# First weight tile ahead of x, an absolute sum traded between VectorE and ScalarE, first convolution ahead of x's statistics, and unread products at TensorE's start

## The chip, the cores and the metric

The kernel runs on one NeuronCore of one Trainium2 chip. Five engines work side by side and meet only at semaphores: TensorE (PE, matmuls and transposes), VectorE (DVE), ScalarE (ACT), GpSimd (POOL), and SyncE (SP), which issues nearly all DMAs. The metric is the device time of one execution in microseconds, as a median over several runs.

## The reference

The computation is one Mamba-like mixer followed by one ternary-weight feed-forward block, on x of shape (4, 512, 512).

```python
# mixer, for each of 4 batches; hidden = ctx (512 x 256), z = layernorm(x)
xi    = in_proj_w @ hidden.T                     # 512 channels x 512 steps
u     = silu(causal_conv(xi, conv_w, 4 taps) + conv_b)
dbl   = x_proj_w @ u                             # dt (16), B (16), C (16)
delta = softplus(dt_proj_w @ dt + dt_proj_b)
state = state * exp(delta * A) + delta * u * B   # 16 states, scan over 512 steps
y     = (sum over states of state * C + D * u) * silu(z)
x     = x + y.T
# feed-forward; x and h are rounded to 8 bits by row
w_q   = clip(round(w / mean|w|), -1, 1) * mean|w|   # w_gate, w_up: 2048 x 512; w_down: 512 x 2048
h     = silu(q(layernorm(x)) @ w_gate_q.T) * (q(layernorm(x)) @ w_up_q.T)
out   = x + q(rms_norm(h)) @ w_down_q.T
```

`mean|w|` is one number for each weight matrix. It needs the sum of the absolute values over the whole matrix before any element can be rounded.

## The kernel before

The kernel has three stages. A preparation stage (0 to about 93 us) makes everything that the scan reads. The scan stage runs 64 steps k (4 batches by 16 states); in each, ACT makes four decay tiles (L697) and four B-scaled tiles (L619 or L622), PE turns them (L1229, L1232), DVE does four scans of 128x512 (L929), POOL multiplies all four by C (L475) and PE adds them up (L1245). The feed-forward stage takes 16 tiles of 128 rows. The changed lines all lie in the preparation stage.

Each engine runs its own list of steps in the order in which it is written. A step that waits on a semaphore holds up all that stands behind it on that engine. The lists of the preparation stage are these.

* **SP** loads in_proj_w, ctx of batch 0, the convolution's constants, x of batch 0 (`load_x(0)`, L270), weight tile (0, 2) (`load_weight(0, 2)`, L276), ctx of batch 1 and so on. Weight tile (w, k) is quarter k of matrix w (0 gate, 1 up, 2 down), 128x2048 float32, 1 MB. Later SP stores the rounded tiles to DRAM (`store_weight`, L283) and waits for each rounded tile first.
* **PE** multiplies in_proj_w with ctx (`conv(b, h)`, L1108, two 128x512 results), adds the partial weight sums over the partitions (`total(w)`, L1158), makes dt, B and C (`project(g)`, L1118, batches 2g and 2g+1), delta's argument (`delta_in`, L1133), and turns z and delta*u (`turn_z` L1142, `turn_du` L1152). All of these but the totals and B share three pairs of PSUM banks: a use of a pair waits until the use three places earlier in `UNIT_USERS` has been read. `keep_warm(n)` (L1163) issues n products of `ones` that nothing reads.
* **ACT** takes the last tap of the convolution out of PSUM (`last_tap`, L558), sums weight tiles (`sum_weight`, L574, with an accumulator read behind it), applies silu to u (`silu_u`, L565, after all of a batch's convolution), scales weight tiles (`scale_weight`, L581, after the mean), keeps B (`keep_bT`, L597), applies softplus (L602) and silu to z (L569).
* **DVE** takes x's statistics (`x_stats(b)`, L872, L875, L877), the other three taps (`conv(b, h)`, L840, 6 instructions), sums some weight tiles (`sum_weight`, L847), turns the totals into means (`mean_weight`, L853, L856, L859), rounds and clips weight tiles (`cut_weight`, L864, L867), and copies the turned delta*u out of PSUM (`keep_duT`, L883).
* **POOL** normalises x (L434, L441) and multiplies delta by u (`du(b)`, L451).

Who sums which tile: ACT sums gate (0,2), (0,1), (0,0), (0,3) and up (1,0), (1,3), (1,1); DVE sums up (1,2) and all four of down. `total(w)` waits on the counters of both engines by the numbers in `ACT_SUMMED` and `DVE_SUMMED`:

```python
def total(w):
    hold(pe, "w_summed_act", ACT_SUMMED[w], "w_summed", DVE_SUMMED[w])
```

On PE `total(1)` stands behind `pe.wait_ge(S["bT_ready"], 1)` (ACT's `keep_bT(0)`) and behind `delta_in(0, 1)`, and ahead of `project(1)`.

Of the kernel before, what the change touches and what calls it, by code (L numbers as in the profile page):

```python
# [68 lines left out]
def mixer_ffn(nc, x, ctx_t, in_t, conv_w, conv_b, xp_t, dt_t, dt_b, a_log, d_skip, w_all, ln_w, out):  # L69
    es = ExitStack()  # L70
    with es:
# [29 lines left out]
        def w_full(at):  # L101
            return part(at, 8)
# [83 lines left out]
        S = {n: sem(n) for n in names}  # L186
# [9 lines left out]
        wq_stored = [[sem(f"w{w}_stored{k}") for k in range(4)] for w in range(2)]  # L196
        LAST = NB * DS - 1

        ACT_SUMMED, DVE_SUMMED = (5, 7, 7), (0, 1, 5)
        DVE_CUT, ACT_CUT = ((0, 0), (0, 3), (0, 1), (0, 2), (1, 1), (1, 0), (1, 2)), ((1, 3),)  # L200

        FFN_STEPS = range(TILES)
# [59 lines left out]
        def _(sp):  # L262
            def load(dst, src, s):
                sp.dma_start(dst, src).then_inc(S[s], 16)
# [4 lines left out]
            def load_x(b):  # L269
                sp.dma_start(gate_rows(b), x_v[:, b, :, :]).then_inc(x_loaded[b], 16)  # L270
# [4 lines left out]
            def load_weight(w, k):  # L275
                sp.dma_start(w_full(W_AT[w][k]), w_all[w * 4 + k, :, :]).then_inc(w_loaded[w][k], 16)  # L276
# [16 lines left out]
            load(cw[:], conv_w.rearrange("(k p) n -> p k n", p=P), "conv_loaded")  # L293
            with nc.allow_non_contiguous_dma("one column for each channel"):
                load(cb[:], conv_b.rearrange("(k p) -> p k", p=P), "conv_loaded")
            load_x(0)
            load_weight(0, 2)
            load_ctx(1)
            load_weight(0, 1)
            load_x(1)  # L300
# [249 lines left out]
        def _(act):  # L550
# [11 lines left out]
            def silu_u(b):  # L562
                act.wait_ge(S["conv_steps"], (b + 1) * 12)
                u = flat(delta_u[:, b, 1])
                nc.scalar.activation(u, u, ACT.Silu).then_inc(S["u_ready"], 1)  # L565
# [6 lines left out]
            def sum_weight(w, k):  # L572
                act.wait_ge(w_loaded[w][k], 16)
                own.done(nc.scalar.activation(w_junk, w_full(W_AT[w][k]), ACT.Abs,  # L574
                                              accum_out=wstat[:, w * 4 + k:w * 4 + k + 1]))
                own.wait()
                act.sem_inc(S["w_summed_act"], 1)
# [17 lines left out]
            def keep_bT(g):  # L595
                act.wait_ge(S["bT_psum"], g + 1)
                nc.scalar.activation(bT[:, 2 * g:2 * g + 2, :, :], ps[:, 7, :].rearrange(  # L597
                    "p (k j n) -> p j k n", k=KL, j=2)[:, :, :, B_AT:C_AT], ACT.Copy).then_inc(S["bT_ready"], 1)
# [26 lines left out]
            act.preload_act_table_set("silu_and_others")  # L625
            last_tap(0, 0)
            last_tap(0, 1)
            sum_weight(0, 2)
            last_tap(1, 0)
            sum_weight(0, 1)  # L630
            last_tap(1, 1)
# [16 lines left out]
            scale_weight(0, 3)  # L648
            sum_weight(1, 1)
            silu_u(2)  # L650
            keep_bT(0)
            silu_u(3)
            act.preload_act_table_set("softplus")
# [158 lines left out]
        def _(dve):  # L812
# [17 lines left out]
            def conv(b, h):  # L830
                v = delta_u[:, b, 1, :, :]
                first = (b * 2 + h) * 6
                for i in range(1, TAPS):
                    for j in range(2):
                        k = 2 * h + j
                        if i == 1:
                            dve.wait_ge(S["tap0_done"], (b * 2 + h) * 2 + j + 1)
                        else:
                            dve.wait_ge(S["conv_steps"], first + (i - 2) * 2 + j + 1)
                        nc.vector.scalar_tensor_tensor(  # L840
                            out=v[:, k, i:], in0=two("conv", b, h)[:, j, 0:L - i],
                            scalar=cw[:, k, TAPS - 1 - i:TAPS - i], in1=v[:, k, i:], op0=ALU.mult,
                            op1=ALU.add).then_inc(S["conv_steps"], 1)

            def sum_weight(w, k):
                dve.wait_ge(w_loaded[w][k], 16)
                nc.vector.tensor_reduce(out=wstat[:, w * 4 + k:w * 4 + k + 1], in_=w_full(W_AT[w][k]), axis=AX.X,  # L847
                                        op=ALU.add, apply_absolute_value=True).then_inc(S["w_summed"], 1)
# [20 lines left out]
            def x_stats(b):  # L869
                dve.wait_ge(x_loaded[b], 16)  # L870
                for k in range(KE):
                    own.done(nc.vector.bn_stats(bst_x[:, k, :], x_all[:, b * KE + k, :]))  # L872
                own.wait()
                for k in range(KE):
                    own.done(nc.vector.bn_aggr(mv_x[:, b, k, :], bst_x[:, k, :]))  # L875
                own.wait()
                nc.vector.tensor_scalar(var_x[:, b, :], mv_x[:, b, :, 1], LN_EPS, None,  # L877
                                        ALU.add).then_inc(S["x_var"], 1)

            def keep_duT(b, h):  # L880
                dve.wait_ge(wq_stored[1][b], 16)
                dve.wait_ge(S["duT_psum"], b * 2 + h + 1)
                nc.vector.tensor_copy(turned[:, b, 2 * h:2 * h + 2, :], two("du", b, h)).then_inc(S["duT_ready"], 1)  # L883

            x_stats(0)
            conv(0, 0)
            conv(0, 1)
            x_stats(1)
            conv(1, 0)
# [5 lines left out]
            conv(2, 1)  # L895
            conv(3, 0)
            conv(3, 1)
            sum_weight(1, 2)
            cut_weight(0, 0)
            mean_weight(1)  # L900
            cut_weight(0, 3)
# [191 lines left out]
        def _(pe):  # L1093
# [66 lines left out]
            def keep_warm(n):  # L1160

                for _ in range(n):
                    mm(ps[:, 6, 0:P], ones[:], ones[:], start=True, stop=True)  # L1163

            pe.wait_ge(S["in_loaded"], 16)
            conv(0, 0)
            conv(0, 1)
# [1 line left out]
            conv(1, 1)  # L1169
            conv(2, 0)  # L1170
            conv(2, 1)
            pe.wait_ge(S["dve_consts"], 1)
            total(0)
            conv(3, 0)
            pe.wait_ge(S["proj_loaded"], 16 * 6)
# [197 lines left out]
```

## Time and profile before

| what | value |
|---|---|
| median of 3 runs | 574.37 us (573.48 to 574.68) |
| profiled execution, span from first to last instruction | 572.7 us |
| profiled execution, a time of its own | not listed; the median run is 1.67 us above this span |
| busy in the span: PE, DVE, ACT, POOL | 536.1, 535.1, 513.3, 465.1 us |
| granted TensorE clock, mean | 0.997 |

Several engines are busy for over 90% of the span, so the busy shares alone do not say which of them sets the time in a given stage. What does are the waits: where an engine has none over a long stretch, it is the bound there or runs level with the bound. Where it has one, the length of that wait is the room that this engine had. A row of the timeline gives the start, the length, the engine, the line and the number of merged instructions; in square brackets stands the idle time just before it and who ended it.

### The profile page before, as it was taken

To read this page: it belongs to the slowest core of one execution; us is meant where nothing else is said; L and a number is where in the kernel's file an instruction comes from. 1 tells how busy PE (TensorE), PEld (TensorE's weight loads), DVE (VectorE), ACT (ScalarE), POOL (GpSimd) and SP (SyncE) were. 2 spreads that over 40 slices of the span, in tenths; PEclk is the share of its full clock that TensorE was granted. 3 is DMA by queue.
4 is the path that set the end of the run, shared out by engine and by line. 5 is a ranking of instruction groups with operands and counts; after the bars stand their busy time and mean duration, and the time that the engine had idled before them with its cause. 6 is when DMAs were issued, how large, how long until landed. Compare 5 with 4: busy or idle time off the path is not lost.

```text
span 572.7 us, 10285 instructions
## 1 busy us (share of the span) xinstructions
PE 536.1 (94%) x3667; PEld 403.2 (70%) x3684; DVE 535.1 (93%) x778; ACT 513.3 (90%) x757; POOL 465.1 (81%) x196
## 2 busy tenths in 40 slices
PE   5888988899999999999999889999899999999996
PEld 2335477799998999989899879998344444444443
DVE  3999988999999999999999999999999999999883
ACT  1899999999999999989999899999987878878784
POOL 4889364999999999999999999995757676675772
PEclk9999999999999999999999998999999999999999
DMA  9992591221111832126632257443544344533521
GB/s 279 408 390 76 201 323 36 55 58 57 56 56 56 191 105 93 56 65 123 165 99 63 59 129 188 137 154 97 83 78 96 76 101 84 110 84 71 106 55 74
DMA packets 62194, 68.64 MB, mean 120 GB/s; under 512 B 41137, under 2 KB 41137, under 8 KB 59969
## 3 DMA queue, kind: packets, MB, share of 16 engines
q1 hardware_dynamic: 59776, 63.59, 37.5%
q0 software_dynamic: 2368, 4.40, 4.8%
q8 instruction: 30, 0.49, 0.4%
q14 instruction: 20, 0.16, 0.1%
HBM read 50.02 MB, written 8.52 MB: 102 GB/s over the span
## 4 chain that ended last, share of the span: by engine, by line
PE 36%; ACT 24%; DVE 18%; POOL 9%; issue 7%; DMA 5%; SPq 0%; DVEq 0%; POOLq 0%
PE ps L1280 16%; ACT arena L697 11%; PE ps L1290 9%; POOL arena L475 9%; ACT arena L622 7%; DVE arena L840 5%; PE ps L1245 4%; PE ps L1229 4%; DMA arena<-c_rows 3%; DVE arena L929 3%; ACT arena L619 2%; PE ps L1232 2%; DVE bst_x L872 2%; DMA arena<-x 1%; DVE arena L864 1%
## 5 line engine op out<-in xcount | busy, mean ns | idle before, releaser
L475 POOL TENSOR_TENSOR arena<-arena 128x2048 f32<-128x2048 f32 x63 | 286.7, 4614 | 14.1 <-DVE arena L929 9.8
L929 DVE TENSOR_TENSOR_SCAN arena<-arena,ps 128x512 f32<-128x512 f32 x256 | 286.7, 1197 | 1.7 <-PE ps L1229 0.4
L697 ACT ACTIVATE arena<-arena,a_neg 128x512 f32<-128x512 f32 x256 | 164.8, 711 | 7.9 <-DVE arena L929 7.8
L1245 PE MATMUL ps<-ident,arena 128*128 128x128 f32 x1024 | 154.8, 274 | 5.9 <-POOL arena L475 3.7
L1245 PEld LDWEIGHTS ps<-ident,arena 128*128 128x128 f32 x1024 | 119.9, 141 | 9.7 <-POOL arena L475 5.3
L1280 PE MATMUL ps<-arena 128*128 128x512 bf16 x497 | 112.5, 379 | 3.6 <-DVE arena L1006 2.2
L1229 PE MATMUL ps<-arena 128*128 128x128 f32 x768 | 103.4, 278 | 3.9 <-DVE arena L929 3.8
L512 POOL TENSOR_TENSOR arena<-arena 128x1024 f32<-128x1024 f32 x30 | 71.0, 2366 | 39.9 <-DVE arena L1006 39.7
L622 ACT ACTIVATE arena<-arena,bT 128x512 f32<-128x512 f32 x160 | 102.0, 710 | 0.0
L1232 PE MATMUL ps<-ident,arena 128*128 128x128 f32 x640 | 96.0, 273 | 3.0 <-ACT arena L622 2.1
L1229 PEld LDWEIGHTS ps<-arena 128*128 128x128 f32 x768 | 94.5, 194 | 5.8 <-ACT arena L622 2.7
L1280 PEld LDWEIGHTS ps<-arena 128*128 128x128 bf16 x512 | 49.7, 98 | 63.6 <-DVE arena L1006 2.7
L1232 PEld LDWEIGHTS ps<-ident,arena 128*128 128x128 f32 x640 | 74.2, 141 | 5.6 <-issue 3.0
L1290 PE MATMUL ps<-arena 128*128 128x512 bf16 x254 | 57.6, 379 | 0.6 <-DVE arena L1079 0.3
L781 ACT ACTIVATE arena<-arena,magic,aq 128x2048 f32<-128x2048 f32 x14 | 29.3, 2095 | 21.9 <-DVE aq L970 21.9
L1290 PEld LDWEIGHTS ps<-arena 128*128 128x128 bf16 x256 | 24.9, 98 | 30.4 <-DVE arena L1079 0.5
L749 ACT ACTIVATE arena<-ps,scales 128x512 f32<-128x512 f32 x64 | 41.8, 678 | 4.0 <-PE ps L1280 3.1
L1006 DVE TENSOR_TENSOR arena<-arena,ps 128x512 f32<-128x512 f32 x64 | 43.5, 681 | 0.6 <-ACT arena L749 0.3
L1108 PE MATMUL ps<-arena 128*128 128x512 f32 x64 | 31.3, 640 | 8.9 <-DMA arena<-ctx_t 8.0
L993 DVE TENSOR_REDUCE half_max<-arena 128x1 f32<-128x1024 f32 x30 | 36.5, 1216 | 2.5 <-DVE var L954 0.5
L441 POOL TENSOR_SCALAR arena<-arena,mv_x,rstd_x 128x512 f32<-128x512 f32 x16 | 33.0, 2076 | 0.4
L840 DVE SCALAR_TENSOR_TENSOR arena<-ps,cw,arena 128x511 f32<-128x511 f32 (+2 forms) x48 | 31.8, 739 | 0.0
(122 smaller groups left out, 574.8 us busy)
## 6 DMA issues: line engine op xcount, KB each, us to landing
arena<-w_all SPq DMA_DIRECT2D x16, 1024.0 KB, 9.2
arena<-c_rows SPq DMA_DIRECT2D x64, 256.0 KB, 3.3
arena<-x SPq DMA_DIRECT2D x4, 1024.0 KB, 16.0
w_ternary<-arena SPq DMA_DIRECT2D x8, 512.0 KB, 4.1
arena<-w_ternary SPq DMA_DIRECT2D x8, 512.0 KB, 4.8
arena<-x POOLq DMA_DIRECT2D x4, 1024.0 KB, 10.6
out<-arena SPq DMA_DIRECT2D x16, 256.0 KB, 2.0
arena<-ctx_t SPq DMA_DIRECT2D x4, 512.0 KB, 14.0
```

The source lines that it names most:

```text
L475: nc.gpsimd.tensor_tensor(hs[:, k % RING, :, :], hs[:, k % RING, :, :], c_bc[:, s:s + 1, :].to_broadcast([P, KE, L]), ALU.mult).then_inc(S ...
L512: nc.gpsimd.tensor_tensor(p2[:, s, w], h2[:, s, w], lnw[:, w], ALU.mult).then_inc(S["p2_ready"], 1)
L622: nc.scalar.activation(dB[:, slot(k), i, :], turned[:, b, i, :], ACT.Copy, scale=bT[:, b, i, n:n + 1]).then_inc(S["dB_ready"], 1)
L697: nc.scalar.activation(dA[:, s, i, :], delta_u[:, b, 0, i, :], ACT.Exp, scale=a_neg[:, i, n:n + 1]).then_inc(S["dA_ready"], 1)
L840: nc.vector.scalar_tensor_tensor(out=v[:, k, i:], in0=two("conv", b, h)[:, j, 0:L - i], scalar=cw[:, k, TAPS - 1 - i:TAPS - i], in1=v[:, k ...
L929: nc.vector.tensor_tensor_scan(out=hs[:, k % RING, i, :], data0=dA[:, k % 2, i, :], data1=ps[:, 4 + i, :], initial=0.0, op0=ALU.mult, op1= ...
L1006: nc.vector.tensor_tensor(h2[:, t % 2, j * 512:(j + 1) * 512], sg[:, j % 2, :], ps[:, U_BANK[(t * 4 + j) % 3], :], ALU.mult).then_inc(S["h ...
L1229: last = mm(to, turned[:, k // DS, c, i * P:(i + 1) * P], dgB[:, slot(k), c, :], start=True, stop=True)
L1232: last = nc.tensor.transpose(to, dB[:, slot(k), c, i * P:(i + 1) * P], ident[:])
L1245: last = mm(ps[:, c, i * P:(i + 1) * P], hs[:, k % RING, i, c * P:(c + 1) * P], ident[:], start=(n == 0 and i == 0), stop=(n == DS - 1), i ...
L1280: last = mm(ps[:, bank, :], q1T[:, t, c, :], w[:, c, j * 512:(j + 1) * 512], start=(c == 0), stop=(c == KE - 1))
L1290: last = mm(ps[:, DOWN_BANK[t % 2], :], q2T[:, t % 2, c, :], wd(c), start=(c == 0), stop=(c == KI - 1))
```

## The change

Five things change.

1. SP issues weight tile (0, 2) ahead of x of batch 0. The two loads trade places; both are 1 MB.
2. The sum of tile (0, 2) moves from ACT (behind its first two `last_tap`) to DVE, as DVE's first step on loaded data.
3. DVE does `conv(0, 0)` ahead of `x_stats(0)`.
4. The sum of tile (1, 2) moves from DVE (behind `conv(3, 1)`) to ACT, between `silu_u(2)` and `keep_bT(0)`. The counts on which `total` waits follow.
5. PE starts with 12 products that nothing reads, once `ones` is set. The wait for it moves from ahead of `total(0)` to the start.

```diff
-        ACT_SUMMED, DVE_SUMMED = (5, 7, 7), (0, 1, 5)
+        ACT_SUMMED, DVE_SUMMED = (4, 7, 7), (1, 1, 5)
@@ SP
+            load_weight(0, 2)
             load_x(0)
-            load_weight(0, 2)
             load_ctx(1)
@@ ACT
             last_tap(0, 0)
             last_tap(0, 1)
-            sum_weight(0, 2)
             last_tap(1, 0)
@@
             sum_weight(1, 1)
             silu_u(2)
+            sum_weight(1, 2)
             keep_bT(0)
             silu_u(3)
@@ DVE
+            sum_weight(0, 2)
+            conv(0, 0)
             x_stats(0)
-            conv(0, 0)
             conv(0, 1)
@@
             conv(3, 1)
-            sum_weight(1, 2)
             cut_weight(0, 0)
             mean_weight(1)
@@ PE
+            pe.wait_ge(S["dve_consts"], 1)
+            keep_warm(12)
             pe.wait_ge(S["in_loaded"], 16)
             conv(0, 0)
@@
             conv(2, 1)
-            pe.wait_ge(S["dve_consts"], 1)
             total(0)
```

## Rows read from the trace of the kernel before

**Rows 1.** The chain that ended last, in order of time: start us, us, what.
```profile
2.80 8.15 DMA arena<-x
10.98 2.48 DVE bst_x L872 x4
54.98 2.19 DVE wstat L847
73.47 4.75 DMA w_ternary<-arena
```

**Rows 2.** DMA issues at 1.2, 2.8 and 3.3 us; last column is us to landing.
```profile
arena<-ctx_t SPq DMA_DIRECT2D x1, 512.0 KB, 4.7
arena<-x SPq DMA_DIRECT2D x1, 1024.0 KB, 8.2
arena<-w_all SPq DMA_DIRECT2D x1, 1024.0 KB, 10.8
```

**Rows 3.** DVE in the timeline, 10 to 182 us.
```profile
10.98 2.47 DVE L872 BATCH_NORM_STATS2 bst_x<-arena 128x6 f32<-128x512 f32 x4 [8.12 <-DMA arena<-x]
...
36.17 4.01 DVE L840 SCALAR_TENSOR_TENSOR arena<-ps,cw,arena 128x511 f32<-128x511 f32 x6
...
57.09 1.22 DVE L864 TENSOR_SCALAR arena<-arena 128x2048 bf16<-128x2048 f32 x1
...
58.95 0.15 DVE L853 TENSOR_REDUCE wsum<-ps 128x1 f32<-128x4 f32 x1
...
91.15 2.36 DVE L883 COPY arena<-ps 128x1024 f32<-128x1024 f32 x2 [0.23 <-PE ps L1152]
...
93.42 82.40 DVE L929 TENSOR_TENSOR_SCAN arena<-arena,ps 128x512 f32<-128x512 f32 x74
```

**Rows 4.** ACT in the timeline, 27 to 175 us.
```profile
27.14 1.91 ACT L574 ACTIVATE arena<-arena 128x2048 bf16<-128x2048 f32 x1 [0.98 <-DMA arena<-w_all]
...
37.64 4.08 ACT L581 ACTIVATE arena<-arena,magic,winv 128x2048 f32<-128x2048 f32 x2
...
50.97 1.89 ACT L574 ACTIVATE arena<-arena 128x2048 bf16<-128x2048 f32 x1
52.77 0.19 ACT L574 ACTIVATION_READ_ACCUMULATOR arena<-arena 128x1 f32 x1
53.08 1.91 ACT L565 ACTIVATE arena<-arena 128x2048 f32<-128x2048 f32 x1
...
56.97 1.28 ACT L653 ACT_TABLE_LOAD   x1
...
82.46 1.03 ACT L569 ACTIVATE arena<-ps 128x1024 f32<-128x1024 f32 x1 [0.88 <-PE ps L1142]
...
90.73 2.56 ACT L697 ACTIVATE arena<-arena,a_neg 128x512 f32<-128x512 f32 x4
...
170.05 2.55 ACT L697 ACTIVATE arena<-arena,a_neg 128x512 f32<-128x512 f32 x4
```

**Rows 5.** All waits of ACT, 27.2 to 96 us: total us, times, longest.
```profile
ACT arena L569 <- PE ps L1142: 0.9, 1, 0.9
ACT arena L602 <- PE ps L1133: 0.3, 1, 0.3
```

**Rows 6.** PE in the timeline, 6 to 92 us.
```profile
6.13 16.62 PE L1108 MATMUL ps<-arena 128*128 128x512 f32 x32 [6.13 <-DMA arena<-ctx_t]
...
57.32 0.35 PE L1158 MATMUL ps<-wstat,ones 128*128 128x4 f32 x2 [0.24 <-DVE wstat L847]
...
88.06 1.06 PE L1152 MATMUL ps<-ident,arena 128*128 128x128 f32 x8 [0.17 <-ACT arena L569]
...
89.95 1.97 PE L1152 MATMUL ps<-ident,arena 128*128 128x128 f32 x16 [0.70 <-POOL arena L451]
```

**Rows 7.** The first convolution's operand loads on PE, a slow and a fast one.
```profile
9.68 0.34 PEld L1108 LDWEIGHTS ps<-arena 128*128 128x128 f32 x1 [0.52 <-issue]
...
12.32 0.19 PEld L1108 LDWEIGHTS ps<-arena 128*128 128x128 f32 x1 [0.24 <-issue]
```

## The prediction

> **What bounds the kernel now.** I read the chain of waits first, from the start to 93 us, because every changed line lies there. The reader is to see that it goes through x's first load, then through DVE with hardly a break from 10.98 to 73.47 us, then through a store of a rounded weight tile [rows 1]. Read alone, it says that DVE sets the preparation stage, and that DVE's wait of 8.12 us for x [rows 3] is the place to put work. The change does that.
>
> The second view is the timeline of ACT, with its waits listed. From 27.14 us, where it waits 0.98 us for weight tile (1,0) [rows 4], to 96 us ACT waits twice: 0.31 and 0.88 us [rows 5]. So ACT is not off the path, it runs one step behind it. The 0.31 us is no room: the product it waits for needs a PSUM pair that ACT's own softplus empties, so that wait moves along with ACT. The room of ACT over 60 us is the 0.88 us ahead of 82.46.
>
> The third view is the start of the scans. DVE scans from 93.42 us without a wait, 74 scans in 82.40 us [rows 3]. ACT is ahead of it there: its first decay tiles start at 90.73, so the first is done near 91.4, 2.0 us before the first scan. The tiles of step 18 start at 170.05 [rows 4], and the scans of step 18 begin two scans before the stretch ends, at 175.8 - 2 x 1.11 = 173.6, so they are ready 2.9 us ahead. DVE's first scan, not ACT's first decay, carries the delay to the end, and behind it nothing has a time of its own that could absorb it: every load and store there is released by scans or products. The price of the change is therefore how far 93.42 moves.
>
> **The change part by part.**
>
> *Loads traded.* x lands at 2.80 + 8.15 = 10.95, tile (0,2) at 3.35 + 10.8 = 14.15 [rows 1, 2]. Both move 1 MB, they land in the order of issue, and the bytes ahead of every later load are the same, so tile (1,0) still lands at 27.1. After the trade (0,2) lands in x's place and x at about 14.15. From 5.9 us (ctx at 1.25 + 4.7) x's megabyte took 5.0 us, beside small loads of constants; the weight's took 3.2. The two bounds of the landing are 5.95 + 3.2 = 9.15, and 14.15 if the trade does nothing. I take 10.75, near the row of x, since the small loads stay where they are.
> The Trainium skill, "DMA: Bandwidth & Descriptors", section "Queues, rings and completion order", says that descriptors of one queue on an engine are consumed in ring order, yet completion is not first in, first out. The two landings, 3.2 us apart in the order of issue [rows 1, 2], agree with the ring order. By ring order alone the traded tile lands near 10.95; if completions slipped past one another, near 14.15, which is the third rival below.
>
> *Sum of (0,2) on DVE, convolution ahead of statistics.* One sum is 2.19 us [rows 1]. DVE starts at 10.75 instead of 10.98 and gets 2.19 longer before everything up to the old place of sum (1,2). So all of it comes 2.19 - 0.2 = 2.0 us later: x_stats, the convolutions, and mean_weight(0), which ends at 36.2 now (the convolution behind it starts at 36.17, rows 3) and at 38.2 then. With x landing at 14.15 and conv(0,0) running to about 16.9, the statistics wait for nothing. The order of the two on DVE is worth zero: the work between them is the same. x's normalisation on POOL is some 3 us later at its end; its reader, turn_z, comes after 70 us, and POOL waits over 8 us before du(0). Zero.
>
> *Sum of (1,2) off DVE.* 2.19 us go from 54.98. So at cut_weight(0,0) DVE stands at 57.09 - 0.2 = 56.9 again: its work from the landing on is what it was, and the wait of 8.12 us is filled with nothing, because it ends where it did. What the trade gives DVE is the 0.2 us by which a weight lands before x did, not 2.19.
>
> *The same sum on ACT.* Taken away: the sum of (0,2) at 16.9 us, 2.1 us. That is ahead of 27.14, where ACT waits for a load; it makes that wait 3.1 us long and gives nothing. Added: the row of another sum and its accumulator read, 53.08 - 50.97 = 2.11 us start to start [rows 4], with one more handover 2.13, at about 55, where ACT has no wait.
> On top of it ACT is late already. scale_weight(0,0) started at 37.64 [rows 4] and now waits for the mean at 38.2 + 0.05, which is 0.6 later. Bounds: 0.1 (the last_tap of conv(2,1) waits for a PSUM pair that DVE empties later) and 0.8 at a landing of 10.95.
> So ACT is late by 0.6 + 2.13 = 2.7 us from keep_bT(0) on, table load at 59.7 instead of 56.97. At 82.46 it had 0.88 of room: 2.7 - 0.88 = +1.85.
>
> *What else waits for ACT's sum.* total(1) on PE ran at 57.32 [rows 6]. Now delta_in(0,1) ahead of it starts when conv(3,1) ends near 57, and takes 1.95 us; the total is done near 59.3. DVE's mean_weight(1) stood at 58.95 [rows 3]: it comes some 0.4 us later. Everything on DVE behind it is 0.4 late, and the cut of (1,2) some 1.2, because ACT scales that tile 2.7 late. Still the copies of delta*u reach their place behind ACT's silu of z, not ahead of it. The last two stores are ready 2.7 us later, the last landing near 86 + 2.7 = 88.7; the copy that needs it stood at 87.8 and moves to 89.6 with PE, so that is covered by less than 1 us.
>
> *From there to the scans.* turn_du(2,1) on PE is released by ACT's silu at 88.06 [rows 6]: +1.85, 89.9. PE's old wait of 0.70 for POOL at 89.95 goes, since du(3) is only some 0.7 late. DVE copies, takes the mean, copies two more; its old wait of 0.23 at 91.15 [rows 3] goes as well. First scan: +1.85 - 0.2 = +1.65, at 95.1.
>
> *Twelve unread products.* The first convolution's eight products run 0.34 + 0.52 = 0.86 us apart at 9.68 and 0.19 + 0.24 = 0.43 at 12.32 [rows 7]: half speed at first, as of 1.2 GHz against 2.4, though the granted clock reads 1.0 throughout. The twelve (24 instructions) start near 2.75 and end about 7.5; conv(0,0) then starts 1.4 us later but runs at the faster pace and ends near 11 instead of 11.8. Without the speedup it ends at 13.3, the upper bound, and conv(0,1) at 20, when DVE first needs it. DVE is summing until 12.9 and can start then or 0.9 later. I take zero; the cover is DVE's new sum. On conv(1,0) the wait for ctx ends it either way.
>
> Sum, against the profiled span of 572.7: +1.65. The median stands 1.67 above that span, and I carry the difference to it: 574.37 + 1.65 = 576.0 us, slower by 0.3%.
>
> **The rivals.**
> 1. *Small loss.* The tile lands early, at 9.95 or before: mean_weight(0) is then no longer behind ACT, and only 0.1 + 2.13 - 0.88 - 0.2 = +1.15 is left; where the last wait of PE for POOL keeps some of its room, +0.5. Time 574.9 to 575.5. For it: the 3.2 us per MB of the second load. Against it: the small loads take their part in the same slot.
> 2. *Faster.* DVE is the bound after all, as the chain has it, and ACT's room at the z stage is larger than 0.88 because its releaser, PE behind DVE's first copy of delta*u, moves. Place: the silu at 82.46. It decides from ACT's lateness being below its room, that is with 2.13 us or more of room. Then the gain is the earlier landing, up to 10.95 - 9.15 = 1.8, less the 0.4 at mean_weight(1): 573.0. For it: the chain shows DVE for 60 us and names ACT nowhere. Against it: the list of ACT's waits.
> 3. *Larger loss.* The loads overlap or slip and tile (0,2) lands up to 14.15: every 1 us later adds 1 us through mean_weight(0) and through DVE alike. At 12.5: 576.0 + 1.75 = 577.8.
>
> **How the numbers follow.** Forecast 60% (its own range 575.5 to 576.8), first rival 22%, second 10%, third 8%. A measurement can tell this kernel from no change at about 0.2%, 1.15 us. Forecast and third rival are slower, less what falls below 575.5: 0.66. The first rival and that remainder are the same: 0.24. Faster: 0.10. The range of 8 in 10 reaches down into the first rival and up to a landing half a microsecond late: 574.3 to 577.2.
>
> **What would show it.** On DVE the first sum starts at 10.5 to 11.0, not at 9. ACT's wait for tile (1,0) is 3.1 us and still ends at 27.1. scale_weight(0,0) starts near 38.3, behind DVE's mean. The softplus table load is at 59.7. The silu at 82.46 stands at 84.3 with no wait ahead of it. The first scan is at 95.1, and DVE has no wait for 74 scans behind it. I am wrong if ACT still waits for PE ahead of that silu, if DVE's first sum starts before 10 us, or if 93.42 moves and the end does not.

## The result and the profile after

The changed kernel takes 577.89 us (median of 5 runs, 576.61 to 578.45) against 574.37 before: ratio 1.0054, 95% interval 1.0035 to 1.0074. By the medians it is slower by 3.5 us, by the ratio by 3.1 (2.0 to 4.3), where 1.65 was forecast, and it lies above the range of 574.3 to 577.2. Two later measurements of the same kernel gave 1.0043 (1.0028 to 1.0057) and 1.0053 (1.0037 to 1.0068). Three single executions in a slow state, of only_warm (794 us), filled_nowarm (802 us) and before_filled (1131 us), count in the medians below and not in the ratios; without them these medians are 575.54, 576.42 and 575.61.

DVE in the timeline of the kernel after. It answers to [rows 3].

```profile
10.22 2.29 DVE L847 TENSOR_REDUCE wstat<-arena 128x1 f32<-128x2048 f32 x1 [7.36 <-DMA arena<-w_all]
...
37.80 4.01 DVE L840 SCALAR_TENSOR_TENSOR arena<-ps,cw,arena 128x511 f32<-128x511 f32 x6
...
56.53 1.22 DVE L864 TENSOR_SCALAR arena<-arena 128x2048 bf16<-128x2048 f32 x1
...
58.87 0.16 DVE L853 TENSOR_REDUCE wsum<-ps 128x1 f32<-128x4 f32 x1
...
94.99 3.43 DVE L929 TENSOR_TENSOR_SCAN arena<-arena,ps 128x512 f32<-128x512 f32 x3
...
177.62 2.46 DVE L939 TENSOR_TENSOR arena<-ps,arena 128x512 f32<-128x512 f32 x4
```

ACT in the timeline of the kernel after, which answers to [rows 4].

```profile
26.46 1.91 ACT L574 ACTIVATE arena<-arena 128x2048 bf16<-128x2048 f32 x1 [0.97 <-DMA arena<-w_all]
...
37.99 4.08 ACT L581 ACTIVATE arena<-arena,magic,winv 128x2048 f32<-128x2048 f32 x2 [0.38 <-DVE winv L859]
...
59.43 1.28 ACT L653 ACT_TABLE_LOAD   x1
...
83.91 1.04 ACT L569 ACTIVATE arena<-ps 128x1024 f32<-128x1024 f32 x1
...
88.78 1.94 ACT L569 ACTIVATE arena<-ps 128x1024 f32<-128x1024 f32 x2 [0.30 <-PE ps L1142]
...
92.61 2.56 ACT L697 ACTIVATE arena<-arena,a_neg 128x512 f32<-128x512 f32 x4
```

The reader is to see three things. First, up to the first scan the forecast holds in this trace: DVE's first sum starts with the landing of the tile at 10.2; cut_weight(0,0) stands at 56.5, where it stood at 57.1; the table load comes at 59.43 (forecast 59.7), the silu of z at 83.91 with no wait ahead of it (84.3), the first scan at 94.99 (95.1). Second, ACT gets a new wait of 0.30 at 88.78. Third, gate 0, the first four L939 behind 74 scans (where DVE takes up the finished scans of batch 0), stands at 177.62. Before, it stood at 175.74. So 1.57 us at the first scan have become 1.88. That is what the first decay lost: 92.61 against 90.73.

One sign of the prediction did not come: ACT's wait for tile (1,0) is 0.97 and ends at 26.46, where 3.1 and 27.1 were expected. ACT waits some 2 us each for PE's convolution ahead of 15.24 and 18.70 instead, where the moved sum had stood.

The new wait of 0.30 comes in part from a store. Chain of waits of the kernel after (start us, us, what):

```profile
75.68 10.60 DMA w_ternary<-arena
86.30 1.24 DVE arena L883
87.54 0.14 issue
87.67 1.08 PE ps L1142 x8
88.78 1.94 ACT arena L569 x2
```

The store of tile (1,1) took 10.6 us, 7.8 before. DVE's copy waits for it, PE's turn of z for the bank that the copy empties, ACT's silu for the turn. The copy waits only 0.18 of these 0.30 for the store: ahead of it stands DVE's sum of tile (2,3), which waited 1.26 us at 83.83 for its load (8.8 us, 7.1 before).

The rest of the loss of this trace builds up behind gate 0. The milestones below are read from each kernel's timelines of ACT and DVE: first decay (L697), first scan (L929), gate 0 (first L939). "Rest" is the span less gate 0, "fall" the time at which the granted clock of TensorE went to half (0.50) ahead of 110 us. Each fall lasts 3.4 us, that of both_late at 97.2 lasts 6.8. The recorded expectations below speak of falls at 23, 28 and 78 us; by the granted clock in stretches of 0.2 us they stand at 25.4, 30.4 and 80.8. A time of its own has each traced execution but the first: the span of before_2 is 573.2 and its time 575.34, 0.8 above its median; by the same 2.1 us between span and time the first trace of before, 572.7, belongs to a time near 574.8 (an estimate), so neither is of a faster execution.

| kernel | first decay | first scan | gate 0 | rest | time of that run | fall |
|---|---|---|---|---|---|---|
| before | 90.73 | 93.42 | 175.74 | 396.96 | | |
| before_2 | 90.97 | 93.67 | 175.98 | 397.22 | 575.34 | |
| after | 92.61 | 94.99 | 177.62 | 398.68 | 578.45 | 25.4 |
| c_after | 93.36 | 95.73 | 178.38 | 397.32 | 577.80 | 30.4 |
| after_3 | 92.84 | 95.22 | 177.87 | 397.03 | 577.01 | |
| only_warm | 93.64 | 96.02 | 179.33 | 398.37 | 579.80 | 80.8, 108.2 |
| no_warm | 92.69 | 95.08 | 177.70 | 396.40 | 576.27 | |
| no_warm_2 | 94.25 | 96.62 | 179.66 | 395.54 | 577.35 | 32.2, 107.3 |
| only_move12 | 91.67 | 94.05 | 177.36 | 396.24 | 575.63 | 105.8 |
| act_late | 92.39 | 93.34 | 177.39 | 396.01 | 575.54 | |
| dve_late | 90.61 | 95.62 | 177.87 | 395.93 | 575.99 | |
| both_late | 94.07 | 96.87 | 179.39 | 396.11 | 577.75 | 80.2, 97.2 |
| filled | 92.37 | 94.75 | 177.79 | 396.51 | 576.42 | 105.4 |
| filled_2 | 92.63 | 95.01 | 177.65 | 395.95 | 575.76 | |
| filled_nowarm | 93.02 | 95.40 | 178.04 | 395.56 | 575.76 | |
| both_dve | 95.12 | 97.55 | 180.14 | 396.86 | 579.14 | 83.9 |
| stats_first | 94.59 | 96.96 | 180.08 | 397.62 | 579.83 | 32.7, 107.8 |
| before_filled | 90.22 | 92.92 | 175.75 | 398.85 | 576.75 | 103.5 |
| before_split | 90.67 | 93.37 | 175.69 | 397.81 | 575.67 | |
| filled_split | 92.38 | 94.75 | 177.40 | 399.70 | 579.22 | |

Where the rest varies can be read from POOL. It multiplies by rows of C that a DMA brings, and waits for some of them. POOL of the kernel after, then of the kernel before:

```profile
203.77 9.08 POOL L475 TENSOR_TENSOR arena<-arena 128x2048 f32<-128x2048 f32 x2 [1.78 <-DMA arena<-c_rows]
213.68 13.60 POOL L475 TENSOR_TENSOR arena<-arena 128x2048 f32<-128x2048 f32 x3 [0.83 <-DMA arena<-c_rows]
```
```profile
201.71 49.80 POOL L475 TENSOR_TENSOR arena<-arena 128x2048 f32<-128x2048 f32 x11 [1.57 <-DMA arena<-c_rows]
```

From gate 0 to gate 1 (the next group of L939, at 250.37 before and 253.60 after) the 20 traces take 73.5 to 76.0 us. Less the waits of POOL for rows of C in that stretch, 19 of them take 73.0 to 73.2, and only_warm 74.7. From gate 1 to gate 2 (the third group, at 326.24 and 330.02), less these waits, 17 traces take 74.6 to 74.7. From gate 2 to the end all take 246.2 to 246.6, but before_filled and filled_split 248. In the first trace of after these waits are 2.9 us between gates 0 and 1, in the kernel before 1.6: that is the 1.35 by which this stretch is longer. The other two traces of the changed kernel have 2.0 and 1.8, before_2 has 0.5, and filled, filled_2 and filled_nowarm have 0.7, 1.0 and 0.9.

### The profile page after: what moved, and what is told of

Read it like the earlier page. It is cut to its first block, busy times and chain, and to the rows that moved or that the text cites. A ratio compares the mean times of both kernels' runs of the same rounds, so it can differ in the third digit from the quotient of the medians.

```text
span 576.3 us, 10350 instructions
## 1 busy us (share of the span) xinstructions
PE 542.1 (94%) x3708; PEld 408.1 (71%) x3708; DVE 537.0 (93%) x778; ACT 513.7 (89%) x757; POOL 470.6 (82%) x196
## 4 chain that ended last, share of the span: by engine, by line
PE 36%; ACT 26%; DVE 17%; POOL 9%; issue 6%; DMA 5%; DVEq 0%; POOLq 0%
PE ps L1281 16%; ACT arena L697 12%; PE ps L1291 9%; POOL arena L475 9%; ACT arena L622 8%; DVE arena L840 5%; PE ps L1246 3%; DMA arena<-c_rows 3%; DVE arena L929 3%; PE ps L1230 3%; ACT arena L619 2%; DMA w_ternary<-arena 2%; PE ps L1233 2%; DVE bst_x L872 2%; DVE arena L864 1%
## 5 line engine op out<-in xcount | busy, mean ns | idle before, releaser
L929 DVE TENSOR_TENSOR_SCAN arena<-arena,ps 128x512 f32<-128x512 f32 x256 | 287.1, 1197 | 3.0 <-PE ps L1230 1.2
L697 ACT ACTIVATE arena<-arena,a_neg 128x512 f32<-128x512 f32 x256 | 165.1, 710 | 9.5 <-DVE arena L929 9.5
L1230 PEld LDWEIGHTS ps<-arena 128*128 128x128 f32 x768 | 93.3, 192 | 5.1 <-ACT arena L619 1.9
L1291 PEld LDWEIGHTS ps<-arena 128*128 128x128 bf16 x256 | 24.8, 98 | 30.4 <-DVE arena L1079 0.5
```

The lines of the kernel that those rows point to most:

```text
L697: nc.scalar.activation(dA[:, s, i, :], delta_u[:, b, 0, i, :], ACT.Exp, scale=a_neg[:, i, n:n + 1]).then_inc(S["dA_ready"], 1)
L929: nc.vector.tensor_tensor_scan(out=hs[:, k % RING, i, :], data0=dA[:, k % 2, i, :], data1=ps[:, 4 + i, :], initial=0.0, op0=ALU.mult, op1= ...
L1230: last = mm(to, turned[:, k // DS, c, i * P:(i + 1) * P], dgB[:, slot(k), c, :], start=True, stop=True)
L1291: last = mm(ps[:, DOWN_BANK[t % 2], :], q2T[:, t % 2, c, :], wd(c), start=(c == 0), stop=(c == KI - 1))
```

## The experiments

Theories, by the letters that the expectations use: **R**, what stands behind the first scan is rigid and the surplus is scatter. **L**, the scan stage amplifies. **A**, ACT and not DVE carries the first block. **C**, TensorE's clock falls in the preparation stage. **W**, the 12 first products cost time. Ratios are to the kernel before on the same chip, with 95% intervals, from five rounds each.

### The changed kernel again, and parts of it

c_after has no edit. only_warm is the kernel before with

```diff
+            pe.wait_ge(S["dve_consts"], 1)
+            keep_warm(12)
             pe.wait_ge(S["in_loaded"], 16)
```

(the same wait ahead of total(0) goes), and no_warm is the changed kernel without these two lines. only_move12 is the kernel before with

```diff
-        ACT_SUMMED, DVE_SUMMED = (5, 7, 7), (0, 1, 5)
+        ACT_SUMMED, DVE_SUMMED = (5, 8, 8), (0, 0, 4)
@@ ACT
             silu_u(2)
+            sum_weight(1, 2)
@@ DVE
-            sum_weight(1, 2)
             cut_weight(0, 0)
```

SP's waits on the number of finished sums are lowered by one with it.

> The changed kernel once more, nothing edited: how far the milestones of a second profiled execution agree. In the first one the first scan stands 1.57 us later than before, gate 0 (first L939) 1.88, gate 1 3.23, gate 2 3.78, the end 3.6. Theory R (behind the first scan all is rigid, and the 2 us gained there are the scatter of one execution's loads): first scan near 95.0 again, but gate 1 anywhere from 252 to 254, and a median between 575.5 and 578. Theory L (the scan stage amplifies the delay, because ACT's decay tiles are late by more than DVE's scans): gate 1 at 253.6 within 0.3 again, median 577.9 within 0.4.

> The kernel before, with only the 12 unread products at TensorE's start. By the prediction's step: first scan moves by 0, time 574.4 (within 0.3 of before). A rival, theory W: products ahead of the first convolution lower TensorE's clock later (in the changed kernel the granted clock reads 0.67 from 24 to 28 us, in the kernel before 1.0) and cost time: the convolution at 24 us takes 5.4 instead of 3.7 us and the time rises by 0.5 to 2 us.

> The changed kernel without the 12 unread products, the wait for the constants back at its old place. Prediction's step: same time as the changed kernel within 0.3, and the granted clock at 24 to 28 us may or may not drop. Theory W: 0.5 to 2 us faster than the changed kernel, clock 1.0 at 24 us.

> The kernel before, with only the sum of weight tile (1,2) moved from DVE to ACT (ACT now sums all eight tiles of gate and up, DVE none); loads, first steps and TensorE's start as before. DVE has 2.19 us less, ACT 2.13 more, so by the prediction's terms scale_weight(0,0) stays at 37.64, the silu of z at 82.46 moves by 2.13 - 0.88 = 1.25, the first scan by 1.05. Theory R: time 574.4 + 1.05 = 575.4. Theory L: first scan 94.5, then 0.3 to 2 more by gate 1, time 576 to 577.5. A rival that DVE alone sets the stage: first scan 1.5 to 2 us earlier than 93.42, time 572.5.

Measured: c_after 577.40, 1.0043 (1.0028 to 1.0057), only_warm 575.63, 1.0030 (1.0007 to 1.0052), no_warm 578.14, 1.0051 (1.0032 to 1.0070), only_move12 576.03, 1.0022 (1.0011 to 1.0033).

c_after decides nothing between R and L: its gate 1 at 253.46 and its median lie inside what R allowed and within 0.1 of what L asked for.

only_move12 gives the ACT term alone. Its first decay is 0.94 later (forecast by the prediction's terms 1.25), its first scan 0.63 (1.05). A sum that DVE gave away made the kernel 1.3 us slower. The rival that DVE alone sets the stage is dead. only_warm did not stay at zero, and its rise lies in what W expected. In its trace ACT waits 3.99 us for PE at 85.38 instead of 0.88, and the clock is down from 80.8 to 84.3 while PE makes what ACT waits for. Stretch of only_warm (us, engines' busy time, then granted clock, DMA share, GB/s):

```profile
72.00:86.00 14.00, 9.87 (x72) 9.28 (x71) 9.63 (x8) 9.98 (x9) 7.56 (x2) 0.88 0.93 324
```

0.88 of 14 us is 1.7 us of full speed lost. Its runs lie in two groups, seven from 573.6 to 575.7 and four from 577.7 to 579.8 (the trace is of the upper one). no_warm shows that the 12 products are not what makes the changed kernel slow: without them it is no faster.

### One engine late at a time

act_late adds an unread sum on ACT, dve_late one on DVE, both_late has both, to the kernel before.

```diff
@@ ACT
             silu_z(3, 1)
+            own.done(nc.scalar.activation(w_junk, flat(delta_u[:, 0, 0]), ACT.Abs, accum_out=ssq_end[:]))
+            own.wait()
@@ DVE
+            dve.wait_ge(S["delta_ready"], 1)
+            step(nc.vector.tensor_reduce(out=half_max[:, 0:1], in_=flat(delta_u[:, 0, 0]), axis=AX.X, op=ALU.add,
+                                         apply_absolute_value=True))
             def scan(k):
```

> The kernel before, with one more absolute sum on ACT (128x2048, about 2.1 us, its result is read by nothing) right ahead of the table load for the decays: ACT's first decay moves from 90.73 to 92.9, DVE's and PE's work ahead of the scans does not move. Theory of the prediction (DVE's first scan carries the delay; ACT is 2.0 us ahead there): first scan 93.5, gate 0 (first L939, 175.74 before) within 0.3 of before, time 574.5 to 574.8. Theory A (ACT is what the first block of scans runs behind, as the chain of waits had it; in three traces gate 0 moved by exactly what the first decay moved): first scan 93.5, gate 0 at 177.9, time 576.5.

> The kernel before, with one more absolute sum on DVE (128x2048, 2.19 us, read by nothing) right ahead of the first scan: first scan moves from 93.42 to 95.6, ACT's first decay stays at 90.73. Theory of the prediction: gate 0 later by 2.19, time 576.6. Theory A: the delay is used up by the lead that ACT regains on DVE in 18 steps; gate 0 later by less than 1 us, time 574.4 to 575.4.

> The kernel before with both unread sums: about 1.7 us on ACT ahead of its first decay and 2.2 us on DVE ahead of its first scan. If gate 0 is the later of first decay + 85.0 and first scan + 82.3 (both engines level, no room on either): first decay 92.4, first scan 95.6, gate 0 at 177.9, time equal to either alone, 575.9 to 576.6. If the lags add: gate 0 at 179.5, time 578.

Measured: act_late 576.15, 1.0023 (1.0011 to 1.0034); dve_late 576.46, 1.0038 (1.0015 to 1.0062); both_late 577.46, 1.0047 (1.0033 to 1.0062). ACT's first decay and DVE's timeline of act_late:

```profile
92.39 2.56 ACT L699 ACTIVATE arena<-arena,a_neg 128x512 f32<-128x512 f32 x4
...
93.34 5.67 DVE L931 TENSOR_TENSOR_SCAN arena<-arena,ps 128x512 f32<-128x512 f32 x5
...
177.39 2.46 DVE L941 TENSOR_TENSOR arena<-ps,arena 128x512 f32<-128x512 f32 x4
```

The first scan did not move, and gate 0 came 1.65 later, by as much as the first decay (1.66). This refutes the prediction's step that DVE's first scan alone carries the delay. dve_late moved gate 0 by 2.13, as the prediction's step has it, with the first decay unmoved, so theory A is wrong too in its strong form. In the kernel before both engines arrive together: first decay + 85.0 = 175.7 and first scan + 82.3 = 175.7, and the later of the two counts. Every trace of the table without a fall from 90 us to gate 0 obeys this within 0.1; in the seven with a fall between 97 and 109 us gate 0 comes 0.2 to 0.7 later than by this rule. both_late came out at gate 0 and in time (179.39 and 577.46) as its rival had it, by which the lags add. Its trace says otherwise: the clock fell at 80.2, ACT waited 2.66 us for PE at 83.92, and with it the first decay is 3.34 late and not 1.7; 94.07 + 85.0 = 179.1 and 96.87 + 82.3 = 179.2. So the later of the two fits and their sum does not, but no trace of both_late without a fall confirms it.

The link that was overlooked is PE. All of its waits on ACT from 95 to 180 us, in act_late and then in the kernel before:

```profile
PE ps L1234 <- ACT arena L622: 3.2, 2, 2.9
PE ps L1231 <- ACT arena L619: 2.7, 1, 2.7
```

```profile
PE ps L1232 <- ACT arena L622: 2.1, 4, 1.1
```

The decay tiles were 2 to 3 us ahead of the scans, as read. ACT's other tiles, the B-scaled ones, go through PE first. PE is late by what ACT is late, and from there works nearly without a gap (busy for 29.6 of the 30 us from 120 to 150 in act_late and for all 26 from 150 to 176), so it does not catch up. DVE's scans, one every 1.111 us, begin to slip at scan 12 in act_late and have lost 1.65 by scan 50. No single wait is long enough for the list of waits to show it.

### Idle stretches of TensorE

filled is the changed kernel with

```diff
             conv(1, 1)
+            keep_warm(7)
             conv(2, 0)
+            keep_warm(12)
             conv(2, 1)
@@
             turn_xdbl(0)
-            keep_warm(6)
+            keep_warm(12)
```

filled_nowarm is the same without the 12 at the start (the wait for the constants ahead of the 7); before_filled is the kernel before with 7 and 3 in the first two places and 10 instead of 3 ahead of turn_du(0, 1). both_dve is the changed kernel with `sum_weight(1, 2)` back on DVE, behind `conv(3, 1)`, and the counts of sums adapted.

> The changed kernel with more unread products in TensorE's idle stretches: 7 ahead of conv(2,0), 12 ahead of conv(2,1), 12 instead of 6 behind turn_xdbl(0). Theory C (part of the loss is TensorE's granted clock, which in some executions falls to half for some 3.4 us while the preparation stage depends on PE: at 23 us in the changed kernel, at 28 in its second run, at 78 in the one with the products alone): no fall before 60 us, silu of u and decay earlier than in the second run, time 0.5 to 1.5 below the changed kernel and its runs closer together. Theory R (clock falls cost nothing on the median): same as the changed kernel within 0.4.

> The changed kernel with the sum of weight tile (1,2) given back to DVE: DVE sums both (0,2) and (1,2), ACT neither. ACT has 2.13 less from 55 us on, DVE 2.19 more. By the prediction's terms ACT is late by 0.6 at scale_weight(0,0), DVE by 2.0 from 57 to the cut of (1,0): the first copy of delta*u moves by 2.0, PE's turn of z and the silu at 82.46 as well: first decay at 92.7, first scan at 95.2, time 576.2 to 577.5, no better than the changed kernel. If ACT's sum is the whole loss (rival): first decay at 91.3, time 575.

> The kernel with TensorE's idle stretches filled (7, 12 and 12 unread products ahead of conv(2,0), conv(2,1) and delta_in(0,0)), but without the 12 products at the very start. Theory C (what counts is that PE does not stand idle between 22 and 49 us; the 12 at the start only move the first fall of the clock): no fall before 60 us, time within 0.5 of the filled kernel, 575.5 to 576.5. Theory W (the 12 at the start are needed, or harmful): more than 0.6 away from it.

> The kernel before with unread products in TensorE's idle stretches: 7 ahead of conv(2,0), 3 ahead of conv(2,1), 10 instead of 3 ahead of turn_du(0,1), where PE waits 1.85 us for DVE. Theory C: the clock does not fall before 90 us, time equal to before or up to 0.5 faster, since the trace of before shows no fall there either. If products in these places cost something by themselves (an own delay on PE), 0.3 or more slower. Gate 0 by the sum of the two lags: the later of first decay + 85.0 and first scan + 82.3, so 175.7.

Measured: filled 576.08, 1.0016 (1.0006 to 1.0027); both_dve 578.60, 1.0057 (1.0038 to 1.0076); filled_nowarm 576.84, 1.0035 (1.0017 to 1.0054); before_filled 575.69, 1.0021 (1.0005 to 1.0037).

Filling alone takes back more than 1 us of the changed kernel's loss, and the first decay comes at 92.4 to 92.6, both as theory C had it. But the gain is not one of fewer falls: the mean granted clock is 0.9945 over 23 executions of filled and filled_2 and 0.9942 over 17 of the changed kernel, and at a mean clock of 0.994 they average 576.1 against 577.9. Nor does it lie ahead of gate 0, where their traces stand at 177.7 and 178.0 on the average. By the traces it lies between gates 0 and 1 (75.3 us on the average in the changed kernel, 73.9 filled), where they show POOL waiting less for rows of C when filled (0.7 and 1.0 us against 2.9, 2.0 and 1.8). Why that wait is shorter, no run shows.

filled_nowarm lies 0.76 above filled by the medians, as W expected, and 0.34 when its 802 us execution is left out, as C expected, so it decides nothing. before_filled is not faster but 1.2 us slower, as the rival of its expectation had it: its first decay is 0.5 earlier, a fall of the clock at 103.5 us takes that back, gate 0 is where it was (175.75), and the rest of that run is 1.9 us longer, 1.7 of it behind gate 2. So more products are no remedy by themselves. both_dve is no better than the changed kernel, as expected, but lies above its expected 576.2 to 577.5, and its size can't be used: the clock fell at 83.9 us, ACT waited 3.40 us for PE at 86.85 and its first decay is at 95.1, where 92.7 was expected.

### Once more, for what was open

before_2, after_3, no_warm_2 and filled_2 repeat the kernels named, all on one chip.

> The kernel before, unedited, for a second trace. Scatter as the cause: its rest behind gate 0 (396.96 in the first trace) differs by a microsecond or more, its first decay by less than 0.3. Otherwise both agree within 0.5.

> The changed kernel, unedited, for a third trace. Theory C (falls of the clock in the preparation stage): either a fall before 100 us and a first decay later than 92.6, or none and the time at the lower end, 576.3 to 577. Theory W (first 12 products lengthen the rest): rest behind gate 0 above 397.3 again.

> The changed kernel without the 12 first products, for a second trace and a firmer median (578.14 of 6 runs, from 576.27 to 579.62). Theory C: median 576.5 to 578, first decay at 92.7 without a fall of the clock before 100 us and later with one. Theory W: rest behind gate 0 below 396.6 again and a median at least 0.7 below the changed kernel's on this chip.

> The changed kernel with its idle stretches on PE filled, for a second trace: Theory C: first decay at 92.4 again, no fall of the clock before 60 us, median 1 us or more below the changed kernel's on this chip. Scatter: no difference from it beyond 0.5.

Measured: before_2 574.53, 0.9999 (0.9986 to 1.0012); after_3 577.78, 1.0053 (1.0037 to 1.0068); no_warm_2 578.62, 1.0068 (1.0050 to 1.0086); filled_2 576.24, 1.0017 (1.0001 to 1.0033). On this chip the kernel before has a median of 575.14 over 22 further executions. after_3 and filled_2 came as theory C had them; no_warm_2 did in its first decay and not in its median, where C expected at most 578.0 and W a median below the changed kernel's. The stretch from 20 to 34 us in before, after, c_after, after_3, no_warm_2 and filled_2 (columns: us, busy time and count of PE, PE's loads, DVE, ACT, POOL, granted clock, DMA share, GB/s):

```profile
20.00:34.00 14.00, 10.78 (x26) 4.42 (x25) 13.93 (x27) 12.66 (x15) 12.47 (x7) 1.00 1.03 403
```
```profile
20.00:34.00 14.00, 10.84 (x21) 4.22 (x20) 13.93 (x27) 12.62 (x14) 13.78 (x8) 0.88 1.03 401
```
```profile
20.00:34.00 14.00, 9.31 (x18) 3.70 (x17) 13.93 (x27) 12.66 (x14) 13.78 (x8) 0.88 1.02 400
```
```profile
20.00:34.00 14.00, 9.11 (x22) 3.65 (x21) 13.93 (x27) 12.77 (x14) 13.78 (x8) 1.00 1.03 401
```
```profile
20.00:34.00 14.00, 9.08 (x19) 3.55 (x18) 13.90 (x31) 13.43 (x15) 13.20 (x8) 0.94 1.03 401
```
```profile
20.00:34.00 14.00, 13.63 (x60) 8.38 (x59) 13.93 (x27) 12.65 (x14) 13.77 (x8) 1.00 1.03 402
```

PE was busy for 10.8 us of these 14 before, in the changed kernel at full clock for 9.1, and for 13.6 when filled. The clock fell at 25 to 33 us in three of five traces of the changed kernel with and without the 12 products, in none of two of before and none of two filled. Over all 20 traces it fell there in 4 of the 7 that have DVE's early sum and are not filled, in none of the 4 filled ones with that sum and in none of the 9 without it. Why PE idles more: conv(2,1) waits until DVE has read conv(1,0), and DVE is 2 us late from the added sum. PE of no_warm_2, and the second of its rows in after_3:

```profile
24.56 3.67 PE L1108 MATMUL ps<-arena 128*128 128x512 f32 x8 [1.67 <-DVE arena L840]
31.49 5.37 PE L1108 MATMUL ps<-arena 128*128 128x512 f32 x8 [3.25 <-DVE arena L840]
```
```profile
30.84 3.67 PE L1108 MATMUL ps<-arena 128*128 128x512 f32 x8 [3.20 <-DVE arena L840]
```

Before, PE waited 0.65 us ahead of conv(2,1). Here it waits 3.25, the clock falls at 32.2, the same eight products take 5.37 us instead of 3.67, ACT waits 2.93 for them at 36.90, and the first decay comes at 94.25, 1.5 later than in the trace without a fall. In after_3 PE waits 3.20 at the same place and the clock stays at full. In c_after a fall at 30.4 us cost 0.5 to 0.7; in the first trace of after one at 25.4, behind an idle stretch of 1.90 us that the kernel before has too (1.91), cost nothing visible.
The Trainium skill, "TensorE: Matmul & The Clock Gate", Part 1, says that a hardware monitor sets the clock between 1.2 and 2.4 GHz by how busy PE has been recently. By that rule longer idle stretches cost clock. The traces agree in part: behind 3.25 us of idle time the products took 5.37 / 3.67 = 1.46 times their length, behind 3.20 us in after_3 they took their full-clock length.

What goes with a fall on the average can be read from the kernel before: over 114 executions, 57 with a mean granted clock of 0.997 average 574.3 us, 53 with 0.993 or 0.994 average 575.2. One fall lowers the mean clock by 0.003 (1.7 us of 573), so one more fall goes with about 1 us. The mean clock is 0.9954 over all 114 and 0.9942 over the 17 of the changed kernel: 0.4 falls more, and by this estimate 0.4 us of its loss.

### Order on DVE, and two tries at the scan stage

stats_first is the changed kernel with `x_stats(0)` ahead of `conv(0, 0)`. before_split halves the large loads of the scan stage in the kernel before, filled_split does both to the changed kernel:

```diff
-                    if n >= 4 and n % 2 == 0 and n < 12 and b > 0:
-                        k = n // 2 - 2
+                    if n >= 4 and n < 12 and b > 0:
+                        k, h = n // 2 - 2, n % 2
...
+                c = slice(h * 1024, h * 1024 + 1024)
+                load(dst[:, k, c], wq_dram[w * 4 + k, :, c], s)
```

> The changed kernel with x_stats(0) ahead of conv(0,0) on DVE again. x lands at 13.6, DVE's sum ends at 12.5: DVE waits about 1.1 us for x, everything behind it up to the mean of the gate weights is 1.1 later, ACT's first scale_weight at 39.1 instead of 38.0, first decay at 93.7 to 94.0, time 1.1 above the changed kernel: 578.5 to 579.2. If ACT had room left there: first decay at 92.8, time as the changed kernel.

> The kernel before with the large loads of the scan stage (rounded gate and up tiles, down tiles) issued in two halves, one in each step n from 4 to 11 instead of one whole in every second. POOL waits 4.3 us in five places for rows of C, which stand behind a whole tile in SP's queue and land in 6.0 instead of 3.2 us. Halved, they land in about 4.7. If these waits carry the time: POOL's waits for C under 1.5 us, time 1 to 3 us below before, and less scatter behind gate 0. If DVE and ACT, level with POOL, take up what POOL gains: 0 to 1.

> The changed kernel with both: filled idle stretches and halved loads. If the stretch behind gate 0 is rigid against what stands ahead of it (theory R), the differences add: filled against before (+1.4) plus halved loads against whole ones, so this kernel stays 1.0 to 1.8 behind the kernel before with halved loads. If the two interact: anywhere else.

Measured: stats_first 580.07, 1.0091 (1.0078 to 1.0104); before_split 576.51, 1.0032 (1.0017 to 1.0047); filled_split 578.01, 1.0057 (1.0034 to 1.0079). In stats_first DVE waited 1.19 us for x, as expected, and the kernel lost 2.2 to 2.7 us against the changed one, 1.1 of it expected; its trace has falls at 32.7 and 107.8 us. So the order "convolution ahead of statistics" keeps the traded loads from costing more, by 1.1 us as worked out and by 2.2 to 2.7 as measured, of which the falls can be a part. before_split missed: POOL still waits 4.3 us for rows of C, and the kernel is 1.8 us slower. POOL of before_split, 180 to 400 us:

```profile
POOL arena L480 <- DMA arena<-c_rows: 4.3, 3, 2.1
```

filled_split stays 1.5 us behind before_split by the medians, inside the expected 1.0 to 1.8, as it would if what is lost ahead of gate 0 and behind it adds. The two traces do not show that: they stand 1.7 apart at gate 0 and 3.6 at the end. No kernel tried beats the one before.

## Why the prediction was wrong

The direction was right, and so was the mechanism up to the first scan. The size was half of the measured one: two steps behind the first scan failed, and about 1 us of the miss is located but not explained.

* Landing of the traded tile: 2.81 + 7.4 = 10.2, taken 10.75, bounds 9.15 and 14.15. Right, and with it the sentence that filling DVE's wait gains only what the weight lands earlier than x did.
* Mean of the gate weights and ACT's first scale: 37.99, taken 38.25. Right in the first trace; in c_after, with the clock down at 30.4, it is 39.16 and ACT's wait for PE (1.75 us) sets it, not DVE's mean.
* ACT's added sum, 2.11 us start to start without cover: 57.34 - 55.23 = 2.11. Right. Room of 0.88 used up: silu at 83.91, taken 84.3. Right.
* The step "DVE's first scan, not ACT's first decay, carries the delay to the end" failed. I had compared ACT's lead on the decay tiles only, 2.0 and 2.9 us. act_late showed that ACT has no room at all, since its other tiles go through PE. It costs 0.3 us here (1.57 against 1.88 in the first trace). The chain of waits named ACT for this stretch, and I set it aside because DVE showed no wait.
* "The order of the two on DVE is worth zero" was wrong as it stood: with x landing at 13.8, statistics first waits 1.19 us (stats_first). It did not enter the sum, since the changed kernel has the good order.
* Missing from the sum: PE's idle time ahead of conv(2,1). I followed that wait to ACT and priced it at 0.1, but not the falls of PE's clock that go with it in some executions. In a trace with such a fall the first decay is 0.5 to 1.5 later; over all executions it comes to 0.4 us by the count above.
* The step "behind it nothing has a time of its own" failed. POOL's waits for rows of C have: the rest behind gate 0 runs from 395.5 to 399.7 us over the traces, 396.96 and 397.22 before, and most of that follows these waits. In the first trace of after they add 1.3 us between gates 0 and 1. The sum put this term at nothing.

What stays open: at gate 0 the traces of the changed kernel are 1.6 to 2.6 us late, about 2.1 on the average, and on the medians the kernel is 2.6 to 3.5 late. Falls of the clock by count do not fill that gap: five executions of the changed kernel with a mean clock of 0.997, so with one fall (every trace has one between 328 and 351 us), average 577.5, against 574.3 for before at 0.997. What is left, about 1 us, would lie behind gate 0, where the traces vary mostly by POOL's waits for rows of C. But why the change makes these waits longer, or whether it does so on the average, three traces against two do not show: summed over both stretches they are 4.7, 3.2 and 2.8 us after, 3.4 and 3.1 before. That filled has shorter ones (2.6 and 1.7) is seen; no run tested why.

## What to carry to other kernels

Filling an engine's wait for a load with other work gains only if the engine can start earlier than before; here the moved load landed where the old one did. When work moves to an engine with "little idle time", take the room from its waits at the places behind the move, and on every path from it, one through a third engine included; two engines without a visible wait over 80 us can both be the bound, and delaying one at a time by a known amount shows it. Where a delay makes PE idle for microseconds, its clock can fall in some executions (here in 4 of 7 traces), and a difference of 1 to 3 us wants more than one trace and the long waits for loads compared in each before it is put down to a cause.

## What the runs showed of the hardware

POOL's four small instructions at L464 (128x128) took 7.18 us in the changed kernel, 2.36 before. POOL is 3.6 us later there, and they now run beside DVE's rounding of weight tiles, which starts at 56.53. POOL of the kernel after, then of the kernel before:

```profile
58.20 7.18 POOL L464 TENSOR_SCALAR arena<-ident,dsk 128x128 f32<-128x128 f32 x4
```
```profile
54.61 2.36 POOL L464 TENSOR_SCALAR arena<-ident,dsk 128x128 f32<-128x128 f32 x4
```

The other side pays as well: DVE's rounding at 69.54 took 2.31 us instead of 1.22, beside POOL's product from 66.22 to 70.77. Before, where that product ended at 69.76, the same rounding at 69.38 took 1.47.

```profile
69.54 2.31 DVE L864 TENSOR_SCALAR arena<-arena 128x2048 bf16<-128x2048 f32 x1
```

The Trainium skill, "SBUF — State Buffer", section "SBUF: two separate sides", says that DVE in some modes and GpSimd share one pair of ports as an exclusive lock; both rows agree with it.
